# Second attention stage: other orders for the last nine steps on VectorE, ScalarE and TensorE

## The reference, cut to what matters

```
h = _layernorm(x, axis=-1) * (1 + ca) + sa
Q, K, V = h @ Wq.T, h @ Wk.T, h @ Wv.T        # as (b, s, 16 heads, 16)
scores = einsum('bshd,bstd->bsht', Q, K) / sqrt(16)
attn = softmax(scores, axis=-1)               # 16 x 16 per token, over heads
out = einsum('bsht,bstd->bshd', attn, V).reshape(b, s, dm)
x = x + ga * (out @ Wfc.T)
h = _layernorm(x, axis=-1) * (1 + cb) + sb    # the normed rows of the experts
logits = h @ Wg                               # 8 experts, a softmax over them
```

## Time and profile before

| what | value |
|---|---|
| median of 3 runs | 1048.13 us (1048.02 to 1050.01) |
| the profiled execution's own time | 1046.45 us |
| its span, first to last instruction | 1044.6 us |
| mean granted clock of TensorE | 0.972 |
| TensorE busy (matmuls) | 960.1 us, 92% |
| VectorE busy | 690.6 us, 66% |
| ScalarE busy | 495.7 us, 47% |
| GpSimd busy | 377.6 us, 36% |

### The profile page before, as it was taken

How to read it: one execution, slowest core, us unless ns; L and a number is a source line. 1 busy time by engine, 2 the same in 40 slices (tenths; PEclk the granted TensorE clock), 3 DMA queues, 4 the chain that set the end, 5 groups by cost and what they waited for, 6 DMA issues and landing times. The chain is left out here.

```text
span 1044.6 us, 30362 instructions
## 1 busy us (share of the span) xinstructions
PE 960.1 (92%) x11177; PEld 824.7 (79%) x11178; DVE 690.6 (66%) x1747; ACT 495.7 (47%) x1343; POOL 377.6 (36%) x330
## 2 busy tenths in 40 slices
PE   6999999989999999999987899999777888999996
PEld 3566665889999999999966788888666878899995
DVE  3478877856777777777412688889986776344442
ACT  3656665404454454454346777776652440322221
POOL 0135334521323323322203556565561101455552
PEclk9999999989999999999998999999968999999999
DMA  9784481394222223222055666766521721444441
GB/s 338 216 329 119 125 276 41 111 379 119 85 92 94 82 87 99 77 91 71 8 108 86 123 124 146 156 133 127 101 67 57 277 97 34 139 134 140 134 136 35
DMA packets 133025, 135.59 MB, mean 130 GB/s; under 512 B 73884, under 2 KB 122142, under 8 KB 130740
## 3 DMA queue, kind: packets, MB, share of 16 engines
q1 hardware_dynamic: 121684, 90.80, 31.4%
q0 software_dynamic: 11232, 43.27, 13.0%
HBM read 96.21 MB, written 44.77 MB: 135 GB/s over the span
## 5 line engine op out<-in xcount | busy, mean ns | idle before, releaser
L1151 PE MATMUL psall<-rows 128*128 128x128 f32 x1872 | 224.0, 277 | 1.4 <-DVE rows L1237 1.4
L1151 PEld LDWEIGHTS psall<-rows 128*128 128x128 f32 x1872 | 218.9, 194 | 2.8 <-issue 1.8
L1114 POOL DMA_INDIRECT x<-ffn_rows,tok_i x78 | 82.8, 1061 | 172.2 <-DVE tok_i L999 69.8
L1165 PE MATMUL psall<-whi,rows 128*128 x624 | 141.0, 379 | 0.0
L1237 DVE COPY rows<-wlo 128x2048 f32 (+2 forms) x78 | 74.1, 950 | 94.9 <-PE psall L1151 85.4
L1165 PEld LDWEIGHTS psall<-whi,rows 128*128 128x128 f32 x624 | 115.7, 190 | 14.1
L1119 POOL DMA_INDIRECT attn_rows<-rows,tok_i x39 | 41.8, 1072 | 183.5 <-DVE rows L1269 183.5
L1497 DVE STREAM_TRANSPOSE whi<-whi 32x512 f32<-32x512 f32 x128 | 89.8, 701 | 9.0 <-POOL whi L1460 7.7
L280 PE MATMUL psall<-cst 128*128 128x128 f32 x714 | 89.9, 283 | 0.5 <-PEq L1380 0.5
L1577 ACT ACTIVATE whi<-psall 32x512 f32<-32x512 f32 x128 | 75.2, 587 | 31.0 <-PE psall L1706 28.4
L1299 ACT ACTIVATE rows<-psall,vs 128x128 f32<-128x128 f32 x312 | 84.9, 383 | 9.8 <-PE psall L1151 7.4
(11 more groups left out here) (250 smaller groups left out, 1729.7 us busy)
## 6 DMA issues: line engine op xcount, KB each, us to landing
ffn_rows<-mod_rows SPq DMA_DIRECT2D x2, 4096.0 KB
wlo<-in_W SPq DMA_DIRECT2D x2, 4096.0 KB, 17.8
whi<-in_w SPq DMA_DIRECT2D x5, 1024.0 KB, 8.4
whi<-mod_rows SPq DMA_DIRECT2D x4, 1024.0 KB, 14.0
ffn_rows<-rows SPq DMA_DIRECT2D x8, 512.0 KB
ffn_rows<-x SPq DMA_DIRECT2D x8, 512.0 KB
wlo<-attn_rows SPq DMA_DIRECT2D x32, 128.0 KB, 3.6
v_turn<-wlo SPq DMA_DIRECT2D x32, 128.0 KB, 3.4
```

The source lines that it names most:

```text
L1114: eng.indirect_dma_start(xin[j % DEEP], None, src_d, bass.IndirectOffsetOnAxis(tok_i[:, j:j + 1].bitcast(U32), 0), bounds_check=T, oob_is_ ...
L1151: last = eng.matmul(b_up[t.par][f // 4][:, (f % 4) * P:(f % 4 + 1) * P], w_now[:, c, f * P:(f + 1) * P], inT[t.par][:, c * P:(c + 1) * P], ...
L1165: last = eng.matmul(b_dn[t.par][:, 0:D], hidT[t.par][:, f * P:(f + 1) * P], w_down[:, bass.ds(e, 1), f, :].rearrange("p o n -> p (o n)"), ...
```

## The change

From step 38 on (DRAIN = NT + LAG_QK; queries and keys of the last tile were issued at step 37), VectorE, ScalarE and TensorE each take a third list, `drain_steps`, in project steps too. Lags stay, but for `turn_h`, `keep_h1T`, `logits` and `keep_logits`, which have LAG_H + 1 there: each tile's turn comes a step later. `later` leaves tile 17 out, which had its turn at step 37. Tile 26 is then left for the code behind the loop. `hold_last` moves to the end of TensorE's step and holds for tiles 29 and 30 instead of 30 and 31. GpSimd's and SyncE's lists do not change.

```diff
--- before.py
+++ after.py
@@ -1356,12 +1356,23 @@
         LAG_MX, LAG_EX, LAG_ET, LAG_PV, LAG_Y = 11, 12, 13, 14, 15
         LAG_XLD, LAG_ROW, LAG_X, LAG_H = 14, 16, 19, 20
 
-        def tile_steps(stages, project_steps=None):
+        DRAIN = NT + LAG_QK
+
+        def tile_steps(stages, project_steps=None, drain_steps=None):
 
             for s in range(NT + LAG_Y):
-                for lag, stage in project_steps if project_steps and (s - LAG_Y) % TB == TB - 1 else stages:
+                now = stages
+                if drain_steps and s >= DRAIN:
+                    now = drain_steps
+                elif project_steps and (s - LAG_Y) % TB == TB - 1:
+                    now = project_steps
+                for lag, stage in now:
                     if 0 <= s - lag < NT:
                         stage(s - lag)
+
+        def later(stage):
+
+            return lambda t: stage(t) if t + LAG_H >= DRAIN else None
 
         def done_by(t, lag, other, steps_ago=0):
 
@@ -1523,7 +1534,9 @@
                     ch.do(eng.scalar_tensor_tensor(h, xr[t // TB % 3][:, t % TB, :], mean[:, 0:1], m3[:, 1, :], ALU.subtract, ALU.mult))
                     eng.scalar_tensor_tensor(h, h, rstd, m3[:, 2, :], ALU.mult, ALU.add).then_inc(c_["h"], 1)
                 tile_steps([(LAG_H, norm2), (LAG_ET, turn_exp), (LAG_X, stats_sum), (LAG_MX, max_scores), (LAG_EX, sum_exp),
-                            (LAG_Y, gate_attention)])
+                            (LAG_Y, gate_attention)],
+                           drain_steps=[(LAG_EX, sum_exp), (LAG_ET, turn_exp), (LAG_X, stats_sum), (LAG_MX, max_scores), (LAG_H, norm2),
+                                        (LAG_Y, gate_attention)])
                 norm2(FIRST_LAST - 1)
                 stats_sum(FIRST_LAST)
                 for t in LAST:
@@ -1601,7 +1614,11 @@
                 tile_steps([(LAG_MX, compact((0, 1), False)), (LAG_N, shift_h), (LAG_V, keep_v), (LAG_EX, exps), (LAG_MX, compact((2, 3), True)),
                             (LAG_H, keep_h1T), (LAG_QK, keep_qk), (LAG_PV, keep_oT), (LAG_H, keep_logits), (LAG_X, rstd2)],
                            [(LAG_MX, compact((0, 1, 2, 3), True)), (LAG_N, shift_h), (LAG_V, keep_v), (LAG_EX, exps), (LAG_QK, keep_qk),
-                            (LAG_X, rstd2), (LAG_H, keep_h1T), (LAG_PV, keep_oT), (LAG_H, keep_logits)])
+                            (LAG_X, rstd2), (LAG_H, keep_h1T), (LAG_PV, keep_oT), (LAG_H, keep_logits)],
+                           [(LAG_EX, exps), (LAG_MX, compact((0, 1, 2, 3), True)), (LAG_PV, keep_oT), (LAG_X, rstd2),
+                            (LAG_H + 1, later(keep_h1T)), (LAG_H + 1, later(keep_logits))])
+                keep_h1T(FIRST_LAST - 2)
+                keep_logits(FIRST_LAST - 2)
                 keep_h1T(FIRST_LAST - 1)
                 rstd2(FIRST_LAST)
                 keep_logits(FIRST_LAST - 1)
@@ -1709,13 +1726,17 @@
                 b_unread = ps[7][:, D:D + P]
 
                 def hold_last(t):
-                    if t >= NT - 2:
+                    if NT - 3 <= t < NT - 1:
                         eng.wait_ge(c_["ve"], NT)
                         hold_clock(eng, 12, b_unread)
-                tile_steps([(LAG_N, turn_n), (LAG_V, values), (LAG_QK, queries_keys), (LAG_H, turn_h), (LAG_PV, hold_last), (LAG_PV, weigh),
+                tile_steps([(LAG_N, turn_n), (LAG_V, values), (LAG_QK, queries_keys), (LAG_H, turn_h), (LAG_PV, weigh),
                             (LAG_H, logits), (LAG_S, scores)],
-                           [(LAG_N, turn_n), (LAG_V, values), (LAG_QK, queries_keys), (LAG_Y, project), (LAG_H, turn_h), (LAG_PV, hold_last),
-                            (LAG_PV, weigh), (LAG_H, logits), (LAG_S, scores)])
+                           [(LAG_N, turn_n), (LAG_V, values), (LAG_QK, queries_keys), (LAG_Y, project), (LAG_H, turn_h),
+                            (LAG_PV, weigh), (LAG_H, logits), (LAG_S, scores)],
+                           [(LAG_PV, weigh), (LAG_Y, project), (LAG_S, scores), (LAG_H + 1, later(turn_h)), (LAG_H + 1, later(logits)),
+                            (LAG_PV, hold_last)])
+                turn_h(FIRST_LAST - 2)
+                logits(FIRST_LAST - 2)
                 hold_clock(eng, 6, b_unread)
                 turn_h(FIRST_LAST - 1)
                 hold_clock(eng, 3, b_unread)
```

## The result

The changed kernel takes 1057.54 us (median of 15 runs, 1052.61 to 1060.82) against 1048.13 us before (median of 15, 1046.13 to 1052.91). The ratio is 1.0079, with a 95% interval of 1.0067 to 1.0090: 8.3 us slower by the ratio, where +5.3 us was forecast. The median lies 1.0 us above the range given; by the ratio on 1048.13 it is 1056.4, at the upper end of it.

A forecast was written before the change was run, and what follows sets the result against it. VectorE was taken to bound steps 39 to 41, a TensorE-ScalarE-VectorE loop steps 42 to 46, hold and roots the tail. Terms 1.5 + 2.1 + 0.4 + 1.3 = +5.3 us on 1048.13 gave 1053.4 us, range 1047.3 to 1056.5.

The forecast's parts named there:

- (a): Step 38: exps(26) ahead of compact(27) on ScalarE delays project(23) and scores(28); +1.5 us, bounds 0 and +3.5.
- (b): Steps 39 to 41: VectorE idles 0.7 to 0.8 us per step before sum_exp; +2.1 us, bounds 0 and +3.
- The loop named: Steps 39 to 41: statistics, root, copy, logits, copy, exponential and six handovers, 3.7 us, of which VectorE fills 3.0.
- (c): Steps 42 to 45: wait for norm2(25) replaced by small handovers; -0.3 to weigh(30), +0.7 to project(31), together +0.4 us.
- rival 2: Steps 43 to 45: weigh(31) freed if TensorE idles under 1 us before logits(22); faster, 1045.5 us, chance 0.12.
- (d): Behind project(31): second pair of turn and logits adds 1.7 us, less 0.4 hidden by norm2(27); +1.3 us, bounds 0 and +1.9.
- The rule on gaps: Steps 39 to 41: shorter TensorE gaps would keep the full clock, making the sum that of the first rival.
- rival 1: Drain steps: full clock kept, shorter gaps, project(27) 3.74 and first hold 2.84 us; +1.2, 1049.3 us, chance 0.14.
- Rival 3: Project(23) and project(27) run wholly at half clock, 2 us more each less overlap; +8.3, 1056.4 us, chance 0.12.
- rival 4: Whole stage: the change does nothing, shifts vanish in slack before 803.85; 1048.1 us, chance 0.07.

The follow-up runs named there:

- e4: The changed kernel with the new lists from step 39 on, step 38 keeping its old ones; ratio 1.0050 to the kernel before.
- e2: The changed kernel without the hold of 6 matmuls ahead of turn_h(27) in the tail; ratio 1.0081 to the kernel before.
- e9: The changed kernel with compact ahead of exps in ScalarE's drain list; 1062.89 us, ratio 1.0135 to the kernel before.
- e1: The changed kernel with ScalarE's root (rstd2) last in its drain list, behind the copies of turned row and logits; 1048.34 us, ratio 1.0002 to the kernel before.
- E5: The changed kernel with root last, turn_h and logits ahead of project and scores, the turned row's copy right behind exps, hold awaiting weigh's copy; 1050.47 us, ratio 1.0024.
- e10: The changed kernel with 8 more holding matmuls at the end of TensorE's steps 39 to 42; ratio 1.0040 to the kernel before.
- e7: The changed kernel with the root last on ScalarE and without the two holds of 12 matmuls (tiles 29 and 30); ratio 1.0018 to the kernel before.
- e11: Kernel before with new lists only from step 43, root last, lagging tile caught up in step 45, 8 more holding matmuls in steps 39 to 41; 1039.88 us, ratio 0.9914.
- e12: The kernel before with only 8 extra holding matmuls behind scores in steps 39 to 41, none of the new orders; ratio 0.9996.

## Why the prediction was right, and where it was off

**Sign and mechanism were right; one chain was misnamed.** The forecast was slower, by waits alone and no added work, and the marks named for it were found: compact(27) 7.5 us behind norm2(17) (7.6 forecast), project(23) 10.0 (9.9 forecast, from 748 to 738.1), 4.67 us idle ahead of logits(22) (4 to 5), project(31) 8.4 behind weigh(30) (8.7), two pairs in the tail. VectorE idles 1.57, 0.94 and 0.94 before sum_exp, each above the 0.5 to 0.9 named, and the later marks came late (weigh(30) at 800.65 instead of 799, the routing at 829.15 instead of 826). The size was +9.2 us in the profile against +5.3, term by term:

*(a) Step 38*, +1.5: measured +2.0, confirmed by e4. Project started as late as said and ran 5.96 us instead of 5.42.

*(b) Steps 39 to 41*, +2.1: measured +2.4. The amount was right (a step is 7.45 us, and 7.46 in e2, against 6.6 to 6.8 before), the chain was not: that the amount came out is in part luck. The prediction had the root of the statistics ahead of the copy. In the trace of after that copy (769.02) starts 0.24 us behind the end of the root, but only 0.03 behind that of turn_h, which stands behind scores: exps, compact 2.4, scores 2.09, turn 0.69, copy, logits, copy, exps, together 7.45. The loop named is shorter than that by 0.2 to 0.3 us and takes over when compact is added to it, as e9 shows. E1 took the root out of it, and the step did not shorten but grew by the root's own time, which was then on the chain that bounds. E5 took logits off that chain, and a third, through exps ahead of compact, was just as long. In addition project(27) ran 6.17 us, longer at half clock, instead of the 5.36 of before: +0.8, which stood in no term.

*(c) Steps 42 to 45*, +0.4: measured +0.7. Up to weigh(30) it was +0.3 where -0.3 was forecast (the hold took 4.66 us, above the 2.84 to 4.05 counted), and from there to project(31) +0.4 where +0.7 was. The prediction set 12.7 us of new waits against 13.0 of old and called it even, where e1 shows that 7.1 us of the new ones hang on one place in ScalarE's list, the root ahead of the copy. It had the reason written out under rival 2, and e1 then came near to that (weigh(30) on the heels of turn_exp(30)).

*(d) The tail*, +1.3: measured +3.3, the term that failed most. The pair itself: from the end of project(31) to the hold of 6, 1.31 us before and 3.18 after, +1.9, where the prediction had 1.7. It then took 0.4 off, for norm2(27) hiding some; it hid nothing. The other 1.4 us is the clock: between the end of project(31) and the hold TensorE worked 1.87 of 3.18 us, the granted clock fell to 0.50 from 817 to 820, and the way from the hold of 6 to the next turn was 1.99 us (816.00 to 817.99) instead of 1.49, and from that turn to turn_h(28) 5.08 (to 823.07) instead of 4.14. E10 separates the two: the same tail with the same gaps, at a granted clock of 1.00, is 18.50 us, 1.7 above the kernel before; the fall of the clock adds 1.6. (In e7 the tail is 20.55 us, of which 2.06 are the slower project(31): 18.5 again.) The prediction had let the clock speak on the middle steps only.

Of the 3.9 us that the sum was short of, some 3 are TensorE's clock: 0.5 in project(23), 0.8 in project(27), 1.4 to 1.6 in the tail.

**The rule on gaps.** By the rule on gaps as the prediction took it from the Trainium skill ("TensorE: Matmul & The Clock Gate", section "HAM oscillation — how this bites in real kernels"), the shorter gaps of the new middle steps would have kept the clock. They did not: it fell near 759 us, where no gap since 747.4 had been longer than 1.7 us, and stayed at 0.50 up to 784 us, with gaps of 1.4 and 0.5 us in a step. With part of the gaps filled by holds it came back: in e11 it is 1.00 from 764 to 784 us, in e10 from 771 on, as the rule says for gaps that are closed.

**The rivals.** Full clock in the drain (rival 1) did not come by itself; made to come in part (e10) it is worth 4.1 us, the figure that rival 1 had, but by luck: rival 1 counted on shorter gaps, project(27) and a first hold of 2.84, and in e10 the first hold took 5.47 and part of the gain is in the tail. Rival 2's point of decision was the right one, and e1 put it there by moving one entry. Rival 3 has the time nearest to the measured one (1056.4 us), but not its way: the two projects took 5.96 and 6.17 us and not the 7 that it named. It was right in that the half clock would cost more than the sum had. That the change does nothing (rival 4) is excluded by the interval.

**What stays open.** Whether the chance position of the clock's fall against the stage explains the wide scatter of the runs (1052.6 to 1060.8) was not tried; the 1.6 to 3.3 us between profiles of the same instructions point that way. No run takes all the chains out of the middle steps at once, so what these steps would take without them is not known.

## What to carry to other kernels

When orders are written out by hand, follow each new list around to where it meets itself: an engine that takes its waits in order turns any two stages that stand next to each other into one chain, and the chain that binds can change with every entry moved (three different ones of 7.1 to 7.5 us here). An entry that waits for the newest data, like the root here, did best last in its list where the engine behind it stood idle for it (7.1 us in steps 43 to 46), and cost its own 0.44 us a step there where it came onto the chain that bounds. Reordering paid only in the last four steps, where TensorE waited for norms in the old order. Filling gaps of the matmul engine paid 5.7 us on top of that (e11) and 4.1 us in the changed kernel (e10), and nothing in the kernel before (e12), so try it anew for each order.

## What was not expected of the hardware

TensorE at half clock with its matmuls going on did not come back to full by them: from 760 to 784 us it was busy 18.53 of 24 us at a granted 0.50, and the clock rose only near 786 us, within the 6.17 us of project(27). Eight extra matmuls of 128x128 at the end of a step kept it at 0.93 over the same stretch in e11 (it fell within the first hold, which took 3.26 us for 16 issues, and was back near 764 us; the next took 2.05) and at 0.77 in e10, where the first hold took 3.76 us and the clock came back behind it, near 771 us. And holding matmuls are not free of what they guard against: a hold of 12 behind 2.8 to 5.1 us of idle time took 4.05 (before) to 5.47 us (e10), and with TensorE busy up to it at full clock 2.84 to 2.94; behind the same 1.73 us of idle time it took 2.84 in one profile (before) and 4.23 in another (e12).
